# Row maxima of two heads in one unit: two PSUM banks read by one VectorE instruction, in a one-core attention and mixture-of-experts layer

## The chip, the cores and the metric

The kernel runs on one core of one Trainium2 chip. The metric is the time of one execution on the device in microseconds (us), the median of the runs. TensorE (PE) multiplies matrices into PSUM, VectorE (DVE) and ScalarE (ACT) read PSUM, GpSimd (POOL) works on SBUF, and SyncE (SP) issues the transfers. PSUM has eight banks of 512 float32 columns on 128 partitions. Semaphores order the engines, and each engine runs its own list of instructions in the order in which it is written.

## What is computed

The layer adds to x the output of two attention branches, which both take the layer norm of x, and of a mixture of experts. Each attention branch has 16 heads of width 16, on 2 batches of 2048 tokens, with a causal mask:

```
scores = jnp.einsum('bqhd,bkhd->bhqk', Q, K) / math.sqrt(D_K)
scores = jnp.where(causal, scores, -jnp.inf)
attn = jax.nn.softmax(scores, axis=-1)
out = jnp.einsum('bhqk,bkhd->bqhd', attn, V).reshape(Bx, Sx, N_HEADS * D_K)
```

The change touches only the largest score of each row, which the softmax subtracts before the exponential.

## The kernel before

The program has stages one behind the other: projections (`stage_a`), attention of both branches (`stage_b`, the stage of the change), the output projections and the router, and the experts. `stage_b` works on G = 16 groups of GH = 4 heads of one batch.

For a group there are two kinds of score blocks. **M blocks** (`ROW_BLOCKS`, 160 a group) have 128 queries on the partitions and up to 512 keys along the free axis; their only use is the row maximum. A block is (head h, query tile t, key chunk c). Blocks that lie wholly below the diagonal are full (96 a group, 512 wide); those on the diagonal are masked (64 a group, 16 each of width 128, 256, 384 and 512). The list has heads h and h+1 next to each other for the same t and c, so blocks 2n and 2n+1 have the same width. A pair of heads lies in the two halves of the partitions of `qs` and `ks`. **S blocks** (40 key tiles times 4 heads) have keys on the partitions and queries along the free axis; ScalarE takes their exponential into `probs` (line 654), and TensorE multiplies these with the values, the PV product of a key tile (line 634, eight matmuls into `v_bank`), one for the four heads of the tile.

An M block runs like this: TensorE multiplies into one bank of `m_banks` (line 616), and VectorE takes the maximum, a full block by `tensor_reduce` (line 691), a masked one by a `memset` of one column that carries the wait and a `tensor_tensor_reduce` with the mask added (lines 687 and 688, a CUSTOM_DVE row and a short READ_ACCUMULATOR row in the trace). `m_banks` is a ring of MRING = 4 single banks, `s_banks` a ring of SRING = 3, and `v_bank` is one bank: all eight are in use. TensorE's function `room` makes a block wait until the unit four places ahead of it in the ring has been read (`m_used`).

When a 512-query chunk has its last block, VectorE joins the maxima of the chunk (line 697), POOL splits them into two parts (lines 551 and 553), and TensorE transposes them (the **N unit**, line 622, TURN_AFTER = 8 blocks later) into a bank of the same ring; ScalarE copies it out (line 667), and SP puts it into spare rows of `qs`, so that the S matmul subtracts the maximum itself. There are four N units a group.

The order of TensorE's list comes from a table, `TURNS`, one string for each of the 40 key tiles: digits are the S blocks of the four heads, M is one M block, V a PV product. The M blocks run LEAD = 88 blocks ahead of the S blocks: these 88 come alone before the first S block (about 226 to 272 us of the span), and while group g is in its S blocks, M blocks 88 to 159 of g and then 0 to 87 of g+1 are worked on. VectorE has little else to do in this stage.

## Time and profile before

| | |
|---|---|
| median of 3 runs | 2504.02 us (2492.83 to 2504.38) |
| the profiled execution | 2510.96 us |
| its span, first to last instruction | 2509.3 us |
| `stage_b` in the span | about 226 to 1855 us |
| PE busy, whole span | 2314.4 us (92%) |
| DVE busy, whole span | 1893.4 us (75%) |
| ACT busy, whole span | 1516.1 us (60%) |
| mean granted TensorE clock | 0.913 of 2.4 GHz |

Times of rows are from the start of the span. Matmul rows overlap one another, since two matmuls that use different halves of the partitions run side by side and each row holds the way through the array as well; a PE that reads as busy may still have room. The gaps of VectorE and ScalarE are real gaps.

### The profile page before, as it was taken

What the parts mean: (1) busy time and instruction counts of PE and PEld (TensorE: products, weight loads), DVE (VectorE), ACT (ScalarE), POOL (GpSimd) and SP (SyncE); (2) the same over time, 40 slices, a digit from 0 to 9 for tenths busy, and PEclk for the clock granted to TensorE, in tenths of its full rate; (3) what the DMA queues carried; (4) which work ended last, traced back from release to release, by engine and by line L of the source; (5) the groups of instructions that cost most, each with busy time, mean ns of one, the idle gap of its engine ahead of it and who ended that gap; (6) DMA issues with size and microseconds to landing.
All of it is one profiled execution on the core that took longest, in us unless ns stands there. A gap on an engine that the chain in (4) does not pass through costs nothing. (4 is left out here: it accounts for less than half of the span.)

```text
span 2509.3 us, 45515 instructions
## 1 busy us (share of the span) xinstructions
PE 2314.4 (92%) x16105; PEld 1323.9 (53%) x16105; DVE 1893.4 (75%) x5752; ACT 1516.1 (60%) x3189; POOL 505.8 (20%) x403
## 2 busy tenths in 40 slices
PE   5996999999999999999999999999957788999994
PEld 3553444444444444444444444444426688999994
DVE  3544988989989899899989988998707764666672
ACT  2541577778777778787777777787841102454451
POOL 0000001010110110101100100101005113777773
PEclk9996799989989899899989998998987787999997
DMA  5996405425244154253351551641117323666653
GB/s 166 295 243 194 57 5 70 52 36 70 37 52 61 19 75 54 29 70 43 45 70 26 63 61 19 78 52 28 15 34 223 127 84 103 141 132 136 143 124 85
DMA packets 145316, 214.56 MB, mean 86 GB/s; under 512 B 54560, under 2 KB 108000, under 8 KB 136672
## 3 DMA queue, kind: packets, MB, share of 16 engines
q1 hardware_dynamic: 132832, 195.27, 39.4%
q0 software_dynamic: 12288, 16.79, 5.2%
q8 instruction: 109, 1.79, 0.3%
q14 instruction: 87, 0.71, 0.1%
HBM read 138.43 MB, written 76.02 MB: 85 GB/s over the span
## 5 line engine op out<-in xcount | busy, mean ns | idle before, releaser
L654 ACT ACTIVATE probs<-s_banks 128x512 f32<-128x512 f32 (+3 forms) x2560 | 1184.6, 539 | 359.1 <-PE s_banks L605 200.6
L691 DVE TENSOR_REDUCE rowmax<-m_banks 128x1 f32<-128x512 f32 x1536 | 965.6, 682 | 87.5 <-PE m_banks L616 80.4
L605 PE MATMUL s_banks<-qs,ks 50*128 50x512 f32 (+3 forms) x2560 | 866.4, 437 | 15.7 <-ACT probs L654 9.5
L616 PE MATMUL m_banks<-ks,qs 48*128 48x512 f32 (+3 forms) x2560 | 830.6, 448 | 26.2 <-PEq L89 20.5
L634 PE MATMUL v_bank<-probs,vs 128*32 128x512 f32 (+3 forms) x5120 | 637.8, 572 | 1.0 <-ACT probs L654 0.4
L605 PEld LDWEIGHTS s_banks<-qs,ks 50*128 50x128 f32 x2560 | 422.2, 193 | 400.6 <-ACT probs L654 366.7
L616 PEld LDWEIGHTS m_banks<-ks,qs 48*128 48x128 f32 x2560 | 414.7, 197 | 297.3 <-DVE rowmax L691 137.5
L688 DVE CUSTOM_DVE_ANT_0 unused<-m_banks,c_maskq 128x128 bf16<-128x128 f32 (+3 forms) x1024 | 464.6, 486 | 81.1 <-issue 77.7
L551 POOL CAST nparts<-negmax 128x16 fp32r<-128x16 f32 x64 | 12.6, 197 | 1279.5 <-DVE negmax L697 1279.5
L1402 PE MATMUL e_banks<-w_parts,hid_parts 128*128 128x256 f32 x1536 | 188.8, 284 | 1.2 <-issue 0.5
L1402 PEld LDWEIGHTS e_banks<-w_parts,hid_parts 128*128 128x128 f32 x1536 | 185.4, 192 | 1.9 <-DVE hid_parts L1321 1.1
L634 PEld LDWEIGHTS v_bank<-probs,vs 128*32 128x32 f32 x5120 | 103.6, 110 | 154.7 <-issue 79.3
L1387 PE MATMUL e_banks<-xinT,w_parts 128*128 128x512 f32 x768 | 179.2, 393 | 5.1 <-DVE w_parts L1300 5.1
L577 PE MATMUL s_banks<-c_identb,c_later_col_swapped 64*128 64x64 bf16 x1024 | 181.9, 196 | 0.0
L577 PE MATMUL s_banks<-c_identb,c_later_col 64*128 64x64 bf16 x1024 | 177.8, 196 | 0.0
L1387 PEld LDWEIGHTS e_banks<-xinT,w_parts 128*128 128x128 f32 x768 | 144.5, 190 | 35.0 <-issue 5.5
L1355 ACT ACTIVATE hid_parts<-e_banks,c_b1T 128x512 fp32r<-128x512 f32 x128 | 89.6, 700 | 112.7 <-PE e_banks L1387 102.8
L1321 DVE TENSOR_TENSOR hid_parts<-e_hid,hid_parts 128x512 fp32r<-128x512 f32 x128 | 99.0, 786 | 46.3 <-ACT e_hid L1356 46.1
L558 POOL TENSOR_TENSOR rden<-rden,pv_sb 128x2048 f32<-128x2048 f32 x16 | 72.8, 4551 | 196.8 <-DMA rden<-rec_scratch 196.8
L1272 POOL TENSOR_SCALAR scaled<-eout,slot_gates 128x256 f32<-128x256 f32 x64 | 99.4, 1564 | 63.8 <-DVE eout L1331 63.8
L1278 POOL DMA_INDIRECT sum_scratch<-scaled,sums_of x64 | 106.6, 1666 | 19.1 <-issue 14.6
L577 PEld LDWEIGHTS s_banks<-c_identb,c_later_col 64*128 64x128 bf16 x1024 | 90.5, 96 | 27.7 <-issue 13.5
(181 smaller groups left out, 1823.8 us busy)
## 6 DMA issues: line engine op xcount, KB each, us to landing
w<-in_L_ffn_fc_w SPq DMA_DIRECT2D x32, 1024.0 KB, 5.2
qs<-q_scratch SPq DMA_DIRECT2D x96, 256.0 KB, 8.4
ks<-k_scratch SPq DMA_DIRECT2D x96, 256.0 KB, 10.2
q_scratch<-parts SPq DMA_DIRECT2D x64, 256.0 KB, 4.3
k_scratch<-parts SPq DMA_DIRECT2D x64, 256.0 KB, 4.5
v_scratch<-vt SPq DMA_DIRECT2D x16, 512.0 KB, 7.5
v_in<-v_scratch SPq DMA_DIRECT2D x32, 256.0 KB, 10.9
qs<-mrows SPq DMA_DIRECT2D x512, 2.0 KB
```

The lines of the kernel that those rows point to most:

```text
L577: ins = pe.matmul(bank[:, j * HALF:(j + 1) * HALF], const[mask][rows, :], const["identb"][rows, rows], start=False, stop=j == 1)
L605: ins = pe.matmul(bank, ks[rows, slot, h // 2, k * P:(k + 1) * P], qs[rows, slot, h // 2, q * CH + first:(q + 1) * CH], start=True, stop=n ...
L616: pe.matmul(room(("M", NM * group + n))[:, 0:width], qs[rows, slot, h // 2, t * P:(t + 1) * P], ks[rows, slot, h // 2, c * CH:c * CH + wid ...
L634: ins = pe.matmul(v_bank[rows, first:CH], vs[:, slot, k, rows], probs[:, (n * GH + h) % PR, 0:CH - first], start=k == 0, stop=k == TPC * ( ...
L654: act.activation(probs[:, n % PR, 0:width], s_banks[:, (NS * group + n) % SRING, 0:width], ACT.Exp, scale=SCALE).then_inc(p_ready, 1)
L688: dve.tensor_tensor_reduce(unused[:, h, 0:width], scores, const["maskq"][:, CH - width:CH], 1.0, NEG, ALU.add, ALU.max, out).then_inc(m_us ...
L691: dve.tensor_reduce(out, scores, AX.X, ALU.max).then_inc(m_used, 1)
L1272: pool.tensor_scalar(scaled[:, u, j, :], eout[:, u, j, :], slot_gates[:, TPE * e + j:TPE * e + j + 1], None, ALU.mult).then_inc(weighed, 1)
L1278: pool.indirect_dma_start(out=sum_dram, out_offset=bass.IndirectOffsetOnAxis(ap=sums_of[:, TPE * e + j:TPE * e + j + 1], axis=0), in_=scal ...
L1321: dve.tensor_tensor(hid_parts[:, LO, f, :], hid[:, f % HRING, :], f32(hid_parts[:, HI, f, :]), ALU.subtract).then_inc(hid_split, 1)
L1387: last = pe.matmul(banks[:, HBANK + f % HRING, :], w1_parts[:, a, h, f * P:(f + 1) * P], xinT[:, b, h, :], start=h == 0 and (a, b) == PASS ...
L1402: last = pe.matmul(banks[:, OBANK + n, j * D:(j + 1) * D], hid_parts[:, a, f, tile * P:(tile + 1) * P], w2_parts[:, b, f, :], start=f == 0 ...
```

## The change

Heads h and h+1 of the same tile and chunk become one unit. The ring has two places of two banks each instead of four places of one bank. TensorE issues both matmuls of a unit next to each other; the first waits for the whole place, and only the second adds to `m_ready`. A full unit is read by one `tensor_reduce` over both banks (128 x 2 x 512 in, 128 x 2 out). A masked unit is read by two instructions as before, and only the second adds to `m_used`. An N unit takes a whole place of two banks.

```
MRING, SRING = 2, 3
...
-            if group < G:
-                order.append(("M", group, n))
+            if group < G and n % 2 == 1:
+                order.append(("M", group, n // 2))
...
-        ring.append(("M", block))
+        if block % 2 == 1:
+            ring.append(("M", block // 2))
...
-        m_banks = ctx.enter_context(nc.psum_tensor("m_banks", [P, MRING, CH], F32))
+        m_banks = ctx.enter_context(nc.psum_tensor("m_banks", [P, MRING, 2, CH], F32))
...
-                        h, t, c = ROW_BLOCKS[n]
-                        width = min(CH, (t + 1) * P - c * CH)
...
-                        rows = slice(h % 2 * HALF, h % 2 * HALF + PAIR_ROWS)
-                        pe.matmul(room(("M", NM * group + n))[:, 0:width], qs[rows, slot, h // 2, t * P:(t + 1) * P],
-                                  ks[rows, slot, h // 2, c * CH:c * CH + width], start=True, stop=True).then_inc(m_ready, 1)
+                        banks = room(("M", NP * group + n))
+                        for half in range(2):
+                            h, t, c = ROW_BLOCKS[2 * n + half]
+                            width = min(CH, (t + 1) * P - c * CH)
+                            rows = slice(half * HALF, half * HALF + PAIR_ROWS)
+                            ins = pe.matmul(banks[:, half, 0:width], qs[rows, slot, h // 2, t * P:(t + 1) * P],
+                                            ks[rows, slot, h // 2, c * CH:c * CH + width], start=True, stop=True)
+                        ins.then_inc(m_ready, 1)
...
-                        out = rowmax[:, group % SLOTS, h % 2 * PAIRS + h // 2, t, c:c + 1]
-                        scores = m_banks[:, place[("M", NM * group + n)] % MRING, 0:width]
-                        dve.wait_ge(m_ready, NM * group + n + 1)
+                        out = rowmax[:, group % SLOTS, h // 2:h // 2 + PAIRS + 1:PAIRS, t, c]
+                        banks = m_banks[:, place[("M", NP * group + n)] % MRING]
+                        dve.wait_ge(m_ready, NP * group + n + 1)
                         if c == t // TPC:
                             dve.memset(dve_pause[:, h:h + 1], 0.0)
-                            dve.tensor_tensor_reduce(unused[:, h, 0:width], scores, const["maskq"][:, CH - width:CH], 1.0, NEG,
-                                                     ALU.add, ALU.max, out).then_inc(m_used, 1)
+                            for half in range(2):
+                                ins = dve.tensor_tensor_reduce(unused[:, h + half, 0:width], banks[:, half, 0:width],
+                                                               const["maskq"][:, CH - width:CH], 1.0, NEG, ALU.add, ALU.max,
+                                                               rowmax[:, group % SLOTS, half * PAIRS + h // 2, t, c:c + 1])
+                                if half == 0:
+                                    dve.memset(dve_pause[:, h + 1:h + 2], 0.0)
+                            ins.then_inc(m_used, 1)
                         else:
-                            dve.tensor_reduce(out, scores, AX.X, ALU.max).then_inc(m_used, 1)
+                            dve.tensor_reduce(out, banks[:, :, 0:width], AX.X, ALU.max).then_inc(m_used, 1)
```

The table `TURNS` is not touched, but a unit now stands where the second of its two M blocks stood. The first place is on TensorE, in blocks 52 to 55 of a group, behind two PV products (m_banks rows are M blocks, s_banks<-qs,ks rows are S blocks, v_bank rows a PV product). Before:

```order
L605 MATMUL s_banks<-qs,ks 128x512 [waits p_ready]
L634 MATMUL v_bank<-probs,vs 32x512 [waits p_ready,pv_copied]
L634 MATMUL v_bank<-probs,vs 32x512 x3
L616 MATMUL m_banks<-ks,qs 128x512 [waits m_used]
L605 MATMUL s_banks<-qs,ks 128x512 [waits p_ready] x2
L616 MATMUL m_banks<-ks,qs 128x512 [waits m_used] x2
L605 MATMUL s_banks<-qs,ks 128x512 [waits p_ready]
L634 MATMUL v_bank<-probs,vs 32x512 [waits p_ready]
L634 MATMUL v_bank<-probs,vs 32x512 x3
L605 MATMUL s_banks<-qs,ks 128x512 [waits p_ready]
L616 MATMUL m_banks<-ks,qs 128x512 [waits m_used]
```

After:

```order
L607 MATMUL s_banks<-qs,ks 128x512 [waits p_ready]
L639 MATMUL v_bank<-probs,vs 32x512 [waits p_ready,pv_copied]
L639 MATMUL v_bank<-probs,vs 32x512 x3
L607 MATMUL s_banks<-qs,ks 128x512 [waits p_ready] x2
L620 MATMUL m_banks<-ks,qs 128x512 [waits m_used]
L620 MATMUL m_banks<-ks,qs 128x512
L607 MATMUL s_banks<-qs,ks 128x512 [waits p_ready]
L639 MATMUL v_bank<-probs,vs 32x512 [waits p_ready]
L639 MATMUL v_bank<-probs,vs 32x512 x3
L607 MATMUL s_banks<-qs,ks 128x512 [waits p_ready]
L620 MATMUL m_banks<-ks,qs 128x512 [waits m_used]
L620 MATMUL m_banks<-ks,qs 128x512
```

The first M block of a unit has moved down to the second: two rows with one wait on `m_used`, and the S blocks that stood between them are issued ahead of both.

The second place is on TensorE, around the N unit behind block 71 (line 622 before, 627 now). Before:

```order
L616 MATMUL m_banks<-ks,qs 128x512 [waits m_used]
L622 MATMUL m_banks<-c_ident,nparts 32x128 [waits split_ready,m_used]
L605 MATMUL s_banks<-qs,ks 128x128 [waits p_ready]
L577 MATMUL s_banks<-c_identb,c_later_col_swapped 128x64
L577 MATMUL s_banks<-c_identb,c_later_col 128x64
L605 MATMUL s_banks<-qs,ks 128x512 [waits p_ready,mrows_in1]
L577 MATMUL s_banks<-c_identb,c_later_col 128x64
L577 MATMUL s_banks<-c_identb,c_later_col_swapped 128x64
L616 MATMUL m_banks<-ks,qs 128x512 [waits m_used]
```

After:

```order
L620 MATMUL m_banks<-ks,qs 128x512 [waits m_used]
L620 MATMUL m_banks<-ks,qs 128x512
L627 MATMUL m_banks<-c_ident,nparts 32x128 [waits split_ready,m_used]
L607 MATMUL s_banks<-qs,ks 128x128 [waits p_ready]
L579 MATMUL s_banks<-c_identb,c_later_col_swapped 128x64
L579 MATMUL s_banks<-c_identb,c_later_col 128x64
L607 MATMUL s_banks<-qs,ks 128x512 [waits p_ready,mrows_in1]
L579 MATMUL s_banks<-c_identb,c_later_col 128x64
L579 MATMUL s_banks<-c_identb,c_later_col_swapped 128x64
L607 MATMUL s_banks<-qs,ks 128x512 [waits p_ready]
```

Before, block 72 stands five rows behind the N unit and waits for the unit four places ahead of it, block 69. Now the unit of blocks 72 and 73 comes below the rows shown, behind three S blocks with their masks; the place two ahead of it is that of blocks 70 and 71, the unit just ahead of the N unit.

The third place is on VectorE, in the third query tile of the first chunk (512 keys three times for two heads, then a masked block of 384 for each). Before:

```order
L691 TENSOR_REDUCE rowmax<-m_banks 128x1 [waits m_ready] x6
L687 MEMSET dve_pause 128x1 [waits m_ready]
L688 ISA unused,rowmax<-m_banks,c_maskq 128x384
L688 ISA rowmax 128x1
L687 MEMSET dve_pause 128x1 [waits m_ready]
L688 ISA unused,rowmax<-m_banks,c_maskq 128x384
L688 ISA rowmax 128x1
```

After:

```order
L701 TENSOR_REDUCE rowmax<-m_banks 128x2 [waits m_ready] x3
L692 MEMSET dve_pause 128x1 [waits m_ready]
L694 ISA unused,rowmax<-m_banks,c_maskq 128x384
L694 ISA rowmax 128x1
L698 MEMSET dve_pause 128x1
L694 ISA unused,rowmax<-m_banks,c_maskq 128x384
L694 ISA rowmax 128x1
```

Three instructions over two banks stand for six over one. The masked unit keeps its six rows, and its second `memset` no longer waits.

## Rows read from the trace of the kernel before

**Rows 1.** The page: busy tenths of DVE and the clock, 40 slices of the span.

```profile
DVE  3544988989989899899989988998707764666672
...
PEclk9996799989989899899989998998987787999997
```

**Rows 2.** Windows, one group of heads each: columns as the first row names them.

```profile
core 0: us, PE busy (x) PEld busy (x) DVE busy (x) ACT busy (x) POOL busy (x), PEclk, DMA share, GB/s
758.30:860.50 102.20, 101.20 (x776) 45.71 (x772) 88.20 (x293) 76.48 (x170) 12.63 (x11) 0.90 0.38 49
860.50:956.20 95.70, 94.32 (x776) 43.70 (x772) 87.94 (x293) 76.03 (x169) 12.67 (x11) 0.98 0.40 52
956.20:1058.50 102.30, 101.33 (x776) 45.69 (x772) 88.22 (x295) 76.55 (x170) 12.64 (x11) 0.90 0.38 49
1058.50:1154.20 95.70, 94.32 (x776) 43.68 (x772) 87.91 (x294) 76.02 (x170) 12.67 (x11) 0.98 0.42 52
```

**Rows 3.** The page: groups of instructions; count, busy us, mean ns, idle before, releaser.

```profile
L654 ACT ACTIVATE probs<-s_banks 128x512 f32<-128x512 f32 (+3 forms) x2560 | 1184.6, 539 | 359.1 <-PE s_banks L605 200.6
L691 DVE TENSOR_REDUCE rowmax<-m_banks 128x1 f32<-128x512 f32 x1536 | 965.6, 682 | 87.5 <-PE m_banks L616 80.4
...
L634 PE MATMUL v_bank<-probs,vs 128*32 128x512 f32 (+3 forms) x5120 | 637.8, 572 | 1.0 <-ACT probs L654 0.4
```

**Rows 4.** Groups of VectorE by shape, 300 to 1700 us; columns as in rows 3.

```profile
L691 DVE TENSOR_REDUCE rowmax<-m_banks 128x1 f32<-128x512 f32 x1352 | 850.4, 682 | 76.7 <-PE m_banks L616 70.2
L688 DVE CUSTOM_DVE_ANT_0 unused<-m_banks,c_maskq 128x512 bf16<-128x512 f32 x230 | 151.9, 686 | 11.6 <-issue 11.0
L688 DVE CUSTOM_DVE_ANT_0 unused<-m_banks,c_maskq 128x384 bf16<-128x384 f32 x232 | 120.4, 553 | 1.8
...
L688 DVE CUSTOM_DVE_ANT_0 unused<-m_banks,c_maskq 128x128 bf16<-128x128 f32 x228 | 58.9, 285 | 40.2 <-issue 39.5
```

**Rows 5.** Waits in one group of heads: waiting line <- awaited, us in total, times, longest.

```profile
PEld s_banks L605 <- ACT probs L654: 22.3, 41, 0.8
ACT probs L654 <- PE s_banks L577: 10.2, 15, 1.1
ACT probs L654 <- PE s_banks L605: 9.6, 19, 1.3
...
PEld m_banks L616 <- DVE rowmax L691: 7.2, 11, 0.8
PEld m_banks L616 <- DVE rowmax L688: 6.3, 8, 1.2
...
DVE rowmax L691 <- PE m_banks L616: 3.8, 10, 0.8
```

**Rows 6.** Windows, the lead of 88 blocks; columns as in rows 2.

```profile
226.00:272.00 46.00, 44.24 (x87) 22.80 (x87) 45.02 (x128) 0.27 (x1) 6.47 (x5) 0.50 0.02 4
```

**Rows 7.** Timeline of the lead: start, duration (merged), engine, instruction [idle before].

```profile
239.62 3.07 DVE L691 TENSOR_REDUCE rowmax<-m_banks 128x1 f32<-128x512 f32 x5
...
240.35 0.28 PEld L616 LDWEIGHTS m_banks<-ks,qs 48*128 48x128 f32 x1 [0.32 <-DVE rowmax L691]
```

**Rows 8.** Timeline of VectorE, blocks 40 to 55 of group 9.

```profile
1139.00 3.68 DVE L691 TENSOR_REDUCE rowmax<-m_banks 128x1 f32<-128x512 f32 x6
1142.61 0.55 DVE L688 CUSTOM_DVE_ANT_0 unused<-m_banks,c_maskq 128x384 bf16<-128x384 f32 x1
...
1143.30 0.55 DVE L688 CUSTOM_DVE_ANT_0 unused<-m_banks,c_maskq 128x384 bf16<-128x384 f32 x1
...
1144.23 3.68 DVE L691 TENSOR_REDUCE rowmax<-m_banks 128x1 f32<-128x512 f32 x6 [0.37 <-PE m_banks L616]
1147.83 0.69 DVE L688 CUSTOM_DVE_ANT_0 unused<-m_banks,c_maskq 128x512 bf16<-128x512 f32 x1
```

**Rows 9.** Timeline of TensorE beside it: M blocks and two PV products.

```profile
1140.17 0.49 PE L616 MATMUL m_banks<-ks,qs 48*128 48x512 f32 x1
...
1141.41 0.39 PE L616 MATMUL m_banks<-ks,qs 48*128 48x512 f32 x1
...
1142.73 0.44 PE L616 MATMUL m_banks<-ks,qs 48*128 48x384 f32 x1
...
1143.69 0.50 PE L616 MATMUL m_banks<-ks,qs 48*128 48x512 f32 x2
...
1144.94 1.06 PE L634 MATMUL v_bank<-probs,vs 128*32 128x512 f32 x8
...
1146.28 0.62 PE L616 MATMUL m_banks<-ks,qs 48*128 48x512 f32 x2
...
1147.84 0.73 PE L616 MATMUL m_banks<-ks,qs 48*128 48x512 f32 x2
```

17 lines of the change are left out of this document (9 added, 8 removed).

## The prediction, made before the changed kernel was run

> **What bounds the kernel now.** The page's slices come first: VectorE is at 0.8 to 0.9 from slice 5 to slice 27 and the granted clock is near full there [rows 1]. That is the attention stage, some 1630 of 2509 us, and the only one that the change touches. Next come windows of one group of heads each. A group takes 95.7 us where the granted clock averages 0.98 and 102.2 us where it averages 0.90; VectorE is busy 88 us in both, so it has 8 us of gaps in the quick kind, and ScalarE, busy 76, has 20 [rows 2]. TensorE reads 94 of 95.7, but its rows overlap, so that number proves no bound. The groups of instructions show who has the work: 1536 full blocks at 682 ns on VectorE, 2560 exponentials at 539 ns on ScalarE, and PV products that hold TensorE about 1.0 us each [rows 3, 9]. The waits then show that nobody is the bound alone: in one quick group TensorE's queue waits for ScalarE 22.3 us in 41 places and for VectorE 13.5 us in 19, ScalarE waits for TensorE 19.8 us, and VectorE's reduces wait for TensorE 3.8 us [rows 5]. Three engines with in-order lists are held together by the slack in their rings. So the change has to be judged by two things: VectorE's work, and the slack of the ring of `m_banks`.
>
> **Step 1, the merged reduce: a gain.** A reduce lasts 682 ns alone, but back to back the starts are closer: five in 3.07 us give (3.07 - 0.68) / 4 = 598 ns [rows 7]. What widens it is the slope per column, which the masked blocks give: (686 - 285) / 384 columns = 1.044 ns [rows 4]. 512 columns cost 535 ns, so the fixed part of a start-to-start step is 598 - 535 = 63 ns. No two-bank reduce is in the trace. Its price by the slope is 598 + 535 = 1133 ns against 2 x 598 = 1196: 63 ns saved, 768 times, **-48 us**. Bounds: if the merged form gives up the overlap too, it costs 682 + 535 = 1217 ns, +21 ns a pair, +16 us; and if the whole fixed part of a lone reduce, 682 - 535 = 147 ns, went with each second one, -113 us. I take -48, since the row of back-to-back reduces is the nearest. In the lead of 88 blocks VectorE is busy 45.0 of 46.0 us [rows 6] and the gain is real there: 32 pairs, 2 us of the 48. Elsewhere it counts only where VectorE is what the others wait for. The masked blocks keep their instructions; the second `memset` loses a wait on a block that has come with the first, which is worth nothing.
>
> The Trainium skill (Vector Engine (DVE) Microarchitecture Reference, 5.2 Measured stream behaviour on trn2) gives 1.04 ns a column and about 75 ns an instruction after overlap. The rows agree with the slope and show 63 ns; by the page's figure this term would be an estimated 768 x 75 ns = 58 us instead of 48.
>
> **Step 2, VectorE starts a unit only when its second block is there: a loss.** Before, a block that comes late holds up only itself, and TensorE may be up to four blocks (4 x 0.60 = 2.4 us) ahead. Now the first of two blocks is issued where the second stood, VectorE waits for both, and a place is given back only after 1.13 us. TensorE's wait for room stays at the same point of its list: the second block waited for the second block two pairs back, and so does the unit. What changes is how late TensorE may come. With all places in turn, the room comes 1.13 us before VectorE runs dry, and issue, matmul and start take 0.05 + 0.49 + 0.04 = 0.58 us (240.30 to 240.35 in [rows 7]; a matmul in [rows 9]; 1144.19 to 1144.23 in [rows 8, 9]). That leaves 0.55 us; before it was 3 x 0.60 - 0.58 = 1.2 us. A PV product alone holds TensorE 1.0 us.
>
> I walk one stretch with TensorE's times held as they are. VectorE's blocks 40 to 45 start at 1139.00 and 0.60 apart, 46 and 47 at 1142.61 and 1143.30, 48 to 53 from 1144.23, 54 at 1147.83 [rows 8]. The second blocks are issued at 1140.17 (43), 1141.41 (45), 1142.73 (47), 1143.69 (49), 1146.28 (53) and 1147.84 (55), behind PV products at 1144.94 and at 1146.84 [rows 9]. Unit 42/43 is ready at 1140.17 + 0.49 + 0.04 = 1140.70: VectorE, free at 1140.21, waits 0.49 and ends at 1141.83. Unit 44/45 is ready at 1141.84 and ends at 1142.97; 46/47 ready at 1143.21, a wait of 0.24, two masked blocks of 0.49 each (553 ns less 0.06 that overlap the next), end 1144.19; 48/49 ready at 1144.23, end 1145.36; 50/51 end 1146.49; 52/53 ready at 1146.72, a wait of 0.23, end 1147.85; 54/55 ready at 1147.84 + 0.50 + 0.04 = 1148.38, a wait of 0.53. Block 54 then starts 0.55 us later than before, with the gain of five merged reduces (0.31) already in it: a raw loss of 0.86 us in 9.4 us. The stage has some 1630 - 46 us outside the lead, 168 such stretches: raw +144 us if all of it is passed on. It is passed on only where TensorE waits for VectorE, 19 places a group, one in 5 us [rows 5]; elsewhere TensorE sets the pace and VectorE catches up. Bounds 0 and +144; I take half, **+72 us**, because such a place comes about twice in a stretch and the late starts come in about half of it.
>
> **Step 3, the N unit takes a place of two banks: a loss.** The unit behind an N unit waits for the unit just ahead of it, not for one two further back, so VectorE has nothing to read from the end of the one until the other has gone through TensorE: 0.58 us at least, 64 times, 37 us. At a granted clock of 0.5 it is longer. Part of it stands in the trace already as waiting of VectorE, and part may be hidden as in step 2. Bounds 0 and +37, the middle **+19 us**. The copy-out of N by ScalarE frees its place before the next unit but one is due, so I cost that at nothing; if ScalarE is late by an exponential, 0.5 us, it would show there.
>
> **Step 4, TensorE: at nothing.** The same matmuls are issued. The two of a unit use different halves of the partitions and run together (two in 0.50 us at 1143.69 [rows 9]), as an M block and an S block did before. S blocks move ahead of first blocks; ScalarE has 20 us of gaps a group [rows 2] and gains nothing that the end shows. POOL and SP keep their lists.
>
> **The sum.** -48 + 72 + 19 = +43 us. Against the profiled execution of 2511 us that is 2554. The median of the runs is 7 us lower, so the forecast is 2504 + 43 = **2547 us**, slower.
>
> **Rivals.**
> *The ring hides it* (22%). The late second blocks stand where TensorE, not VectorE, sets the pace, and the faster VectorE is early at the next wait. For it: VectorE's gaps are 8 us of 95.7 and ScalarE's 20 [rows 2], so VectorE's work should count. Against: the 0.55 us of slack against a PV product of 1.0 us. Steps 2 and 3 fall to 19 us or less: 2504 - 48 + 19 = 2475.
> *The terms cancel* (17%): step 2 at 30 us instead of 72, 2504 - 48 + 30 + 19 = 2505.
> *The clock falls more often* (12%). Of the four groups shown, two take 6.5 us longer, with more of their time at the lower level of 1.2 GHz (mean 0.90 of 2.4) [rows 2]; I take it that half of the 16 do. A slower feed of TensorE means more pauses in it, and if they bring the long kind to all groups, 8 x 6.5 = 52 us come on top: 2599.
> The Trainium skill (TensorE: Matmul & The Clock Gate, A second HAM failure mode: psum-queue depth-cycling) tells of a kernel in which short idle times between matmul groups, from cycling through the PSUM queue, made the clock go up and down at a cost in throughput. The trace shows the two kinds of groups, but not that the ring is the cause.
> *The two-bank reduce doesn't do what it should* (4%): it costs 1217 ns or more, so step 1 is +16 instead of -48, and the time is 2504 + 16 + 72 + 19 = 2611.
> The forecast itself, slower by 13 to 117 us through late second blocks, has 45%.
>
> **How the numbers follow.** Low end: the first rival with a little less loss, 2470. High end: step 2 in full and step 3 in full, 2504 - 48 + 144 + 37 = 2637, cut to 2620, since not all waits can be passed on. The forecast's own range is 2517 to 2621. A measurement of this kernel can tell about 0.5% (12.5 us) from no change. Faster: the first rival, 0.22. Within: the second, 0.17. Slower: forecast, clock and price, 0.45 + 0.12 + 0.04 = 0.61.
>
> **What would show it.** Step 1: reduces of 128x2 out, 768 of them, with a mean near 1217 ns (starts 1133 ns apart), and VectorE busy some 50 us less. Step 2: VectorE's reduces waiting for `m_banks` matmuls several times the 3.8 us a group, and quick groups of 97 to 100 us instead of 95.7. Step 3: a gap of about 0.6 us in VectorE behind each of the four N units. If the quick groups take 93 us, the ring hid it and I am wrong; if groups at clock 0.90 are 14 or more, the clock did it.

## The result and the profile after

The changed kernel takes 2661.01 us (2653.39 to 2675.29, four runs) against 2498.67 us (2492.83 to 2504.38, four runs) of the kernel before on the same chip: ratio 1.0656 with a 95% interval of 1.06 to 1.0713. It is slower by 162 us, where the prediction said 43 and at most 117 of the same sign. In some experiments part of a kernel's runs took over 1.5% longer at a lower clock, and the ratios and intervals are of its other runs alone. The profiled execution has 2675.29 us, its span is 2673.6 us (before: 2509.3), its mean granted clock 0.883 (before: 0.913).

The page after, slices of VectorE and of the clock, beside [rows 1]:

```profile
DVE  3536886878778778787787877877832783667662
PEclk9995897979979879898897987988987786999997
```

The clock has a 7 or an 8 in the attention stage about every second slice, and VectorE is at 0.7 to 0.8 instead of 0.8 to 0.9. The page's groups of instructions (count, busy us, mean ns, idle before and what ended it), beside [rows 3]:

```profile
L659 ACT ACTIVATE probs<-s_banks 128x512 f32<-128x512 f32 (+3 forms) x2560 | 1189.5, 538 | 506.2 <-PE s_banks L607 307.0
L701 DVE TENSOR_REDUCE rowmax<-m_banks 128x2 f32<-128x1024 f32 x768 | 921.5, 1221 | 184.8 <-PE m_banks L620 180.9
...
L694 DVE CUSTOM_DVE_ANT_0 unused<-m_banks,c_maskq 128x128 bf16<-128x128 f32 (+3 forms) x1024 | 459.7, 486 | 172.9 <-issue 171.2
```

The 768 merged reduces are there, 1221 ns each, 921.5 us busy instead of 965.6. The idle time ahead of the reduces went from 87.5 to 184.8 us, that ahead of the exponentials from 359.1 to 506.2: VectorE has less to do, ScalarE the same, and both wait longer. Two groups of heads after, windows, beside [rows 2]:

```profile
core 0: us, PE busy (x) PEld busy (x) DVE busy (x) ACT busy (x) POOL busy (x), PEclk, DMA share, GB/s
811.10:919.10 108.00, 105.52 (x780) 46.02 (x772) 85.95 (x246) 76.73 (x169) 12.65 (x11) 0.91 0.37 46
919.10:1029.60 110.50, 108.06 (x780) 47.30 (x772) 86.18 (x246) 76.79 (x169) 12.62 (x11) 0.88 0.35 45
```

Before, a quick and a long kind took turns, 95.7 and 102.2 us. Now all are long, and longer than the long kind was. Waits in two groups after (so halve them), beside [rows 5]:

```profile
PEld s_banks L607 <- ACT probs L659: 51.7, 91, 1.7
ACT probs L659 <- PE s_banks L607: 38.6, 47, 2.4
ACT probs L659 <- PE s_banks L579: 25.2, 35, 2.0
DVE unused L694 <- issue: 22.8, 30, 2.4
DVE rowmax L701 <- PE m_banks L620: 22.8, 35, 1.9
...
PEld m_banks L620 <- DVE rowmax L701: 10.8, 16, 1.7
```

The reduces wait 11.4 us a group instead of 3.8, and the masked pairs (their wait is in the `memset` ahead, so it reads as issue) another 11.4. TensorE waits for ScalarE 25.9 instead of 22.3, and ScalarE for TensorE 31.9 instead of 19.8: the same three engines wait for one another, longer. TensorE's wait for room is the exception: 9.9 us a group for VectorE (10.8 and 9.0 in the window of two groups) instead of 13.5.

This compares groups at different clocks. In the kernel before, the group at 0.90 (956.2 to 1058.5 us) already has 6.3 us of such waiting of the reduces and 25.9 of ScalarE. Like for like is smaller; it is read below from groups at full clock.

**How much of it is the clock.** The clock has two levels, 2.4 and 1.2 GHz, so the time at the lower one is 2 x (1 - mean) x time. Before, the long kind has 20.4 us of it and the quick kind 3.8: 16.6 us more at the low level cost 6.5 us, 0.39 us each. Freed from that, both kinds are 94.2 us (the same for both by construction; the windows give the clock to two digits, so 0.39 is good to a few hundredths). After, the groups have 19.4 and 26.5 us at the low level; less 0.39 times that, they are 100.4 and 100.2. Over 16 groups: 6.1 x 16 = 98 us more at equal clock, and (8.95 - 4.75) x 16 = 67 us for more time at the low level, together 165 us. The two profiled executions differ by 164. This is a split by arithmetic from two groups of each kernel; the experiments test both halves, and the whole stage is split at the end. Where the clock falls, before and after, in windows:

```profile
core 0: us, PE busy (x) PEld busy (x) DVE busy (x) ACT busy (x) POOL busy (x), PEclk, DMA share, GB/s
1000.00:1008.00 8.00, 8.00 (x80) 4.79 (x78) 7.65 (x47) 6.22 (x19) 0.42 (x2) 1.00 1.10 128
1008.00:1028.50 20.50, 20.44 (x91) 7.59 (x89) 12.54 (x45) 11.40 (x22) 5.34 (x4) 0.50 0.21 31
1028.50:1040.00 11.50, 11.08 (x92) 5.01 (x94) 10.42 (x29) 9.53 (x20) 6.04 (x2) 1.00 0.32 48
```

```profile
868.00:877.00 9.00, 8.63 (x61) 3.69 (x61) 8.37 (x24) 8.02 (x18) 1.40 (x3) 1.00 0.38 58
877.00:896.70 19.70, 19.65 (x86) 6.96 (x83) 10.04 (x20) 9.18 (x18) 9.99 (x2) 0.50 0.24 32
...
919.10:972.00 52.90, 51.38 (x419) 23.30 (x411) 44.78 (x143) 40.09 (x91) 1.25 (x6) 1.00 0.56 67
972.00:999.00 27.00, 26.60 (x115) 11.18 (x119) 15.16 (x50) 14.74 (x31) 9.17 (x5) 0.51 0.20 32
```

The first fence is the kernel before: the clock falls at 1008 us, at block 157, among the narrow masked blocks at the end of a group's list. The second is the kernel after: the falls are at 877 and 972 us (blocks 13 and 152), and nearly every group has 20 to 27 us at the low level, where before seven of the sixteen had only about 3. VectorE is busy 61% of a low stretch before and 51 to 56% after: everything slows there.

### The profile page after: what moved, and what is told of

It is laid out like the page before. It is cut to its first block and busy times, and to the rows that moved or that the text cites. A ratio compares the mean times of both kernels' runs of the same rounds, so it can differ in the third digit from the quotient of the medians.

```text
span 2673.6 us, 44747 instructions
## 1 busy us (share of the span) xinstructions
PE 2438.8 (91%) x16105; PEld 1343.4 (50%) x16105; DVE 1863.4 (70%) x4984; ACT 1523.2 (57%) x3189; POOL 504.2 (19%) x403
## 5 line engine op out<-in xcount | busy, mean ns | idle before, releaser
L659 ACT ACTIVATE probs<-s_banks 128x512 f32<-128x512 f32 (+3 forms) x2560 | 1189.5, 538 | 506.2 <-PE s_banks L607 307.0
L701 DVE TENSOR_REDUCE rowmax<-m_banks 128x2 f32<-128x1024 f32 x768 | 921.5, 1221 | 184.8 <-PE m_banks L620 180.9
L607 PE MATMUL s_banks<-qs,ks 50*128 50x512 f32 (+3 forms) x2560 | 847.4, 449 | 14.3 <-ACT probs L659 9.9
L620 PE MATMUL m_banks<-ks,qs 48*128 48x512 f32 (+3 forms) x2560 | 716.2, 466 | 59.9 <-DVE rowmax L701 29.8
L639 PE MATMUL v_bank<-probs,vs 128*32 128x512 f32 (+3 forms) x5120 | 672.1, 600 | 1.0 <-ACT probs L659 0.4
L694 DVE CUSTOM_DVE_ANT_0 unused<-m_banks,c_maskq 128x128 bf16<-128x128 f32 (+3 forms) x1024 | 459.7, 486 | 172.9 <-issue 171.2
L620 PEld LDWEIGHTS m_banks<-ks,qs 48*128 48x128 f32 x2560 | 346.2, 206 | 267.9 <-DVE rowmax L701 114.5
L579 PE MATMUL s_banks<-c_identb,c_later_col 64*128 64x64 bf16 x1024 | 170.8, 198 | 0.0
L579 PE MATMUL s_banks<-c_identb,c_later_col_swapped 64*128 64x64 bf16 x1024 | 168.8, 198 | 0.0
L1331 DVE TENSOR_TENSOR hid_parts<-e_hid,hid_parts 128x512 fp32r<-128x512 f32 x128 | 92.8, 738 | 44.0 <-ACT e_hid L1366 43.7
## 6 DMA issues: line engine op xcount, KB each, us to landing
ks<-k_scratch SPq DMA_DIRECT2D x96, 256.0 KB, 10.2
```

What stands on the lines that cost most here:

```text
L579: ins = pe.matmul(bank[:, j * HALF:(j + 1) * HALF], const[mask][rows, :], const["identb"][rows, rows], start=False, stop=j == 1)
L607: ins = pe.matmul(bank, ks[rows, slot, h // 2, k * P:(k + 1) * P], qs[rows, slot, h // 2, q * CH + first:(q + 1) * CH], start=True, stop=n ...
L620: ins = pe.matmul(banks[:, half, 0:width], qs[rows, slot, h // 2, t * P:(t + 1) * P], ks[rows, slot, h // 2, c * CH:c * CH + width], start ...
L639: ins = pe.matmul(v_bank[rows, first:CH], vs[:, slot, k, rows], probs[:, (n * GH + h) % PR, 0:CH - first], start=k == 0, stop=k == TPC * ( ...
L659: act.activation(probs[:, n % PR, 0:width], s_banks[:, (NS * group + n) % SRING, 0:width], ACT.Exp, scale=SCALE).then_inc(p_ready, 1)
L694: ins = dve.tensor_tensor_reduce(unused[:, h + half, 0:width], banks[:, half, 0:width], const["maskq"][:, CH - width:CH], 1.0, NEG, ALU.ad ...
```

## The experiments

The theory going in (A): the start of a pair is late because VectorE waits for its second block and the ring has too little slack (step 2). Rivals: the coarser release of places (B), the clock (C), the order in which TensorE issues the blocks (D), and the merged instruction itself. Each median stands with that of the kernel before on the same chip.

### One part at a time: wait, release, order, reduce

**The wait alone**, on the kernel before:

```
-                        dve.wait_ge(m_ready, NM * group + n + 1)
+                        dve.wait_ge(m_ready, NM * group + (n | 1) + 1)
```

> The kernel before, with one change: VectorE waits for both blocks of a pair before it reads the first. TensorE's order, the ring of four single banks and the release of each bank are as before. Theory A (the loss is that VectorE starts a unit late; my hand walk gave a raw loss of 0.86 us in 9.4 us, 144 us over the stage, of which some part is passed on): 2530 to 2600. Theory B (the loss is the ring, where room comes for two blocks at once and late): 2499 to 2515, since TensorE still gets each bank back singly. Theory C (the clock: any new gap brings the long low stretch to all groups): 2499 + 52 = 2551 or more, with groups of 102 us and a mean clock near 0.89.

Measured: 2572.82 against 2490.99 us, 1.034 (1.026 to 1.042). Windows, two of its groups:

```profile
686.00:785.80 99.80, 95.74 (x776) 42.77 (x772) 88.37 (x294) 77.05 (x169) 12.66 (x11) 1.00 0.39 50
1086.30:1191.30 105.00, 101.11 (x776) 44.64 (x772) 88.67 (x294) 77.39 (x169) 12.65 (x11) 0.93 0.38 48
```

A group at full clock takes 99.8 us, 5.6 more than 94.2, or 16 x 5.6 = 90 us by estimate, against 82 measured. The mean clock is no lower than before (0.919 to 0.932 against 0.915 to 0.928). So this is a loss of structure (more time at the same clock), not of clock, and waiting for the second block is enough to cause one.

**The wait and the release by pairs**, on the kernel before (the wait as above, and):

```
-                    pe.wait_ge(m_used, ring[n][1] + 1)
+                    pe.wait_ge(m_used, (ring[n][1] | 1) + 1)
```

> As the run that waits for both blocks, and TensorE in addition waits for both blocks of a pair to be read before it takes a bank of that pair. Order of TensorE and single place of the N unit as before. Theory A: within 20 us of the run with the wait alone, because a second block's wait for room is where it was. Theory B: most of the loss appears here, 2560 to 2660. If both theories hold a part, half of the loss each.

Measured: 2884.92 us, 1.1613 (1.1513 to 1.1713), clock 0.867, groups of 116 to 130 us. This is outside what either theory gave. With the blocks still spread over TensorE's list, the coarse release makes the first block of a pair wait for a whole pair, and the ring has little slack of this kind.

**The order alone**: the kernel before, single banks, single waits and releases, the first block issued where the second stands:

```
-            if group < G:
+            if group < G and n % 2 == 1:
+                order.append(("M", group, n - 1))
                 order.append(("M", group, n))
```

> The kernel before, with one change: TensorE issues the first block of a pair where the second stood, right ahead of it; VectorE's reads, the four single banks and their release are as before. Theory A: little, 2490 to 2520, since VectorE can still start with the first block and the second is where it was. A rival D (the order of TensorE's list, tuned for single blocks, is what breaks: two blocks with their weight loads at one point, S blocks ahead of them) expects 2550 or more here.

Measured: 1.0523 (1.0412 to 1.0634), some 130 us. The two runs behind this ratio took 2607.96 and 2634.01 us (clock 0.901 and 0.885), two more 2662.50 and 2666.71 us (0.876 and 0.873). The profile is of the one of 2662.50 us. Two of its groups:

```profile
911.00:1020.10 109.10, 108.15 (x780) 48.09 (x772) 88.31 (x293) 76.78 (x169) 12.64 (x11) 0.87 0.35 46
1020.10:1122.90 102.80, 101.53 (x780) 45.74 (x772) 88.16 (x294) 76.57 (x169) 12.70 (x11) 0.95 0.39 48
```

This is what I had costed at nothing. VectorE's instructions and the ring are as before, and most of the loss is there: some 130 us, with an interval of 103 to 158. By the price of the low clock the two groups are 98.0 and 98.8 us at full clock, some 4 more than before, or 16 x 4.2 = 67 us, and the rest is clock.

**The merged reduce undone**: the changed kernel, with a full unit read by two instructions, the second of which releases.

```
-                            dve.tensor_reduce(out, banks[:, :, 0:width], AX.X, ALU.max).then_inc(m_used, 1)
+                            for half in range(2):
+                                ins = dve.tensor_reduce(rowmax[:, group % SLOTS, half * PAIRS + h // 2, t, c:c + 1],
+                                                        banks[:, half, 0:width], AX.X, ALU.max)
+                            ins.then_inc(m_used, 1)
```

> The changed kernel, with each full unit read by two reduces of one bank instead of one over two banks; only the second releases. It takes the merged instruction away and keeps everything else. Its price by the rows is 598 + 598 against 598 + 535 ns, 63 ns for 768 units, 48 us at most: 2661 + 48 = 2709 if VectorE sets the pace, 2661 if TensorE and ScalarE do. With three engines that wait for each other in turn I expect the middle, 2670 to 2700.

Measured: 2671.15 us, 1.0741 (1.0663 to 1.0819). The changed kernel is at 1.0656: the merged instruction gains 10 us by medians and 21 by ratios, which the overlapping intervals don't separate from nothing. It is not the cause of the loss. With the merge undone the full reduces wait 154.2 us for TensorE in the whole span and the masked ones 137.6; with the merge it is 180.9 and 171.2. In these two profiled executions (2667.28 and 2675.29 us) the merge makes VectorE 41 us less busy (1904.1 to 1863.4), and it waits more than that longer.

**Order, wait and release together, in single banks**: both edits above and the order, on the kernel before. Its N unit takes one bank.

```
+                order.append(("M", group, n - 1))
...
+                    pe.wait_ge(m_used, (ring[n][1] | 1) + 1)
...
+                        dve.wait_ge(m_ready, NM * group + (n | 1) + 1)
```

> The kernel before, with all three: both blocks of a pair issued where the second stood, VectorE waits for both, and TensorE waits for both to be read. It lacks only the merged instruction and the two-bank place of the N unit of the changed kernel. Theory D (the place of the blocks in TensorE's list makes nearly all of the loss; the run with that alone gave 2648): the wait and the release add nothing, since both blocks now come together: 2640 to 2670. Theory A or B (ring and wait add their own loss): 2700 or more. The difference to the changed kernel with two reduces (2671) is the N unit's wide place; my price for it was 19 us, 37 at most.

Measured: 2670.99 against 2487.41 us, 1.0765 (1.0675 to 1.0855). Two groups:

```profile
1469.40:1584.30 114.90, 112.35 (x780) 48.37 (x772) 88.94 (x295) 77.38 (x169) 7.18 (x10) 0.84 0.35 44
1584.30:1684.80 100.50, 97.47 (x780) 43.16 (x772) 88.41 (x293) 76.45 (x169) 7.23 (x10) 1.00 0.39 50
```

The same time as with the wide place for N (2671.15, ratio 1.0741), but this doesn't price the wide place. In single banks the second block behind an N unit waits for the block four places ahead, which belongs to the pair just ahead of the N unit, and the release by pairs makes it wait for all of that pair; VectorE waits for this second block. So the same gap stands here (VectorE, block 72 of a group, at full clock):

```profile
709.03 1.29 DVE L692 TENSOR_REDUCE rowmax<-m_banks 128x1 f32<-128x512 f32 x2 [1.26 <-PE m_banks L617]
710.91 1.29 DVE L692 TENSOR_REDUCE rowmax<-m_banks 128x1 f32<-128x512 f32 x2 [0.59 <-PE m_banks L617]
```

At full clock a group takes 100.5 us, what the arithmetic gave for the changed kernel. The other has 36.8 us at the low level for 14.4 us more: 0.39 again. The parts don't add: the wait alone +5.6 us a group, the order alone about +4, all of it +6.3.

### Other orders

**Both blocks where the first stood**, on the kernel before, and the same on the changed kernel:

```
+            if group < G and n % 2 == 0:
+                order.append(("M", group, n))
+                order.append(("M", group, n + 1))
```

> The kernel before, with both blocks of a pair issued where the first stood, so that the second moves up instead of the first moving down. Everything else as before. Theory D1 (what costs is that the first block comes late and VectorE has nothing to read): the loss goes, 2480 to 2530. Theory D2 (what costs is the clump itself, two blocks and a wait for two banks at one point of TensorE's list with S blocks behind them): as slow as the run with the second's place, 2610 to 2670.

```
-            if group < G and n % 2 == 1:
+            if group < G and n % 2 == 0:
```

> The changed kernel, with a unit where the first of its two blocks stood instead of the second. Theory D1: faster than the changed kernel by what the run on the kernel before gains, 2540 to 2600. Theory B (two places of a ring are too few, wherever the unit stands): unchanged or slower, 2650 to 2750, since TensorE now waits for room earlier and holds up the S blocks behind it.

Measured: 2687.67 and 2696.01 us on the kernel before (two more runs 2735.10 and 2750.56 us; no interval), and 2658.39 us on the changed one (1.0693, 1.0619 to 1.0768). Issuing early doesn't help: the changed kernel is no faster by it, at a higher mean clock (0.901 against 0.883), and the other is slower than with the second's place. So "the first block comes too late" doesn't explain the loss of the order. What both places have in common is two M blocks in a row; that this is the reason is argued, not shown.

**Even turns** on the changed kernel:

```
+TURNS = ("0MM12VMM3",) * 40
```

> The changed kernel with another table: each key tile is 0, unit, 1, 2, PV, unit, 3, so that there are two units in every tile, one PV product between any two tiles' units, and neighbours always in different halves of the partitions. Theory D (only the table doesn't fit the units): 2430 to 2500, VectorE's merged reduce gains its 48 us and the late units go. Theory B (the ring is too short for a PV product of 1.0 us whatever the order): 2560 or more.

Measured: 2847.53 and 2859.81 us (two more runs 2932.13 and 2934.82 us; no interval), clock 0.852 in the profiled one. A regular order is no better; it is some 190 us worse than the irregular table.

**A table placed for units.** Perhaps the table only suits single blocks. I placed a new one with units in mind for the changed kernel, and, as the control, one by the same method for the kernel before. (First turns only; all 40 differ.)

```
-TURNS = ("01MM2M3", "0V1MMM2M3V", "0MMM12V3M",
+TURNS = ("M01M23MM", "012MM3", "MM01MVM2M3",
```

> The changed kernel with another table for TensorE's list, in which the units, the S blocks and the PV products are placed for units of two blocks and two places of room; nothing else is changed, and no tile has the same string as before. Theory D (the loss comes from a table that was made for single blocks): most of it goes, 2480 to 2540, near the kernel before or below it. Theory B (two places are too few for a PV product of 1.0 us, whatever the order): 2600 or more. Since all orders so far gave groups of 99 to 102 us at full clock where the kernel before has about 94, I expect about 96 to 97 here, and the rest is the clock's share.

```
+TURNS = ("M01MM23M", "MM01V2MM3MM", "0VM1M2M3VM",
```

> The kernel before, single blocks and four banks, with a table made in the same way for single blocks. A control: if orders made in this way are simply better, part of what the run with the table for units shows is not owed to the units. If the table of the kernel before is near the best for its ring, 2470 to 2510; if it leaves 2 us a group, 2450 to 2475.

Measured: 2708.42 us in one run and 2811.76 to 2830.51 in three, the profiled one (2811.76) among these, for the changed kernel; 2609.68 us (1.0482, 1.0428 to 1.0536) for the control; against 2490.9. One group of each:

```profile
959.70:1079.10 119.40, 118.83 (x777) 50.97 (x773) 86.17 (x245) 76.28 (x168) 12.62 (x11) 0.76 0.33 42
```

```profile
638.00:743.60 105.60, 101.14 (x772) 45.95 (x772) 88.77 (x293) 76.18 (x168) 12.72 (x11) 0.89 0.37 47
```

The method's own table costs the kernel before 119 us, so it tells nothing of the change itself. With 57 us at the low level, 119.40 would be 97 at full clock by the price of 0.39, less than the 100.3 of the changed kernel, but by the 0.33 measured below for groups that are long at the low level it would be 100.5. So whether the order was better at equal clock stays open, and even the quickest run is 47 us slower than the changed kernel.

### Less work on TensorE

If the loss comes from PV products of 1.0 us being longer than the ring's slack of 0.55 us, halving them should help the changed kernel more than the one before. These two kernels leave out the left half of the columns of the PV products of all key tiles but the first of a chunk (and add a constant in the copy-out).

```
+                        left = max(first, CH // 2) if k > 0 else first
...
-                            ins = pe.matmul(v_bank[rows, first:CH], vs[:, slot, k, rows],
-                                            probs[:, (n * GH + h) % PR, 0:CH - first],
+                            ins = pe.matmul(v_bank[rows, left:CH], vs[:, slot, k, rows],
+                                            probs[:, (n * GH + h) % PR, left - first:CH - first],
```

> The kernel before, with PV products of half the columns: for every key tile but a chunk's first, only the queries 256 to 511 of the chunk are multiplied with the values, so that a PV product holds TensorE about 0.57 us instead of 1.0 (and one is added to every sum, so that it stays finite). It leaves that work out. It is the base for the same edit of the changed kernel. VectorE's 88 us a group are the bound that is left: groups near 91 us, 2400 to 2440.

> The changed kernel, with the same short PV products (that work is left out). The changed kernel loses 170 us to the kernel before with full PV products. Theory A/B (a PV product of 1.0 us against 0.55 us of slack in the ring makes the late units): with 0.57 us the loss falls to half or less, 80 us or less to the kernel before with short products, and were the slack all of it, the merged reduce's 48 us would show as a gain. Theory D (the order, whatever the PV product lasts): the loss stays at 120 to 170 us.

Measured: 2585.08 us (1.0356, 1.0285 to 1.0428; the profiled run 2601.55) on the kernel before, clock 0.808, and 2978.11 us (1.1999, 1.1894 to 1.2105) on the changed one, clock 0.678. Both became slower by doing less, and both times are outside what was expected. Two groups of the first and one of the second:

```profile
779.30:867.50 88.20, 86.44 (x774) 45.06 (x775) 86.37 (x293) 76.24 (x169) 12.68 (x11) 1.00 0.45 56
1278.70:1396.40 117.70, 117.17 (x774) 59.44 (x774) 89.04 (x293) 78.93 (x170) 7.21 (x10) 0.62 0.33 42
```

```profile
910.40:1036.70 126.30, 124.04 (x773) 61.53 (x772) 86.41 (x247) 78.53 (x170) 12.64 (x11) 0.62 0.31 39
```

Where the clock stayed full, short products bring a group of the kernel before from 94.2 (estimated above) to 88.2 us, and VectorE has 1.8 us of gaps left: with short products VectorE is nearly the bound. But the clock fell in most groups and took it all back and more. In the changed kernel no group stayed at full clock (0.55 or 0.62 in all ten that were read), so the question that these two were made for stays open.

### More work on TensorE

If the clock is half of the story, unused columns in the narrow blocks should hold it. VectorE reads what it read.

**Wide**: the masked blocks of query tiles 0 to 7 are multiplied 512 wide.

```
+                        if t < 8:
+                            width = CH
```

> The kernel before, with the masked M blocks of query tiles 0 to 7 (blocks 112 to 159 of a group) multiplied 512 columns wide whatever their mask; VectorE reads the same columns as before. More columns stream through TensorE just where its clock falls once a group (blocks 152 to 157). If the clock falls for want of work there, groups of 102 us (20 us at the low level) become groups of 95 to 97: 2440 to 2480, faster than the kernel before. If it falls for another reason, the added columns only cost: 2495 to 2520.

> The changed kernel with the same wide blocks. A group of it has 20 to 27 us at the low level and takes 108 to 110.5 us; by the kernel before (6.5 us for 17 us more at the low level, 0.38 each) it would take 100.2 at full clock. If the wide blocks keep the clock up, 2661 goes to between 2510 and 2600, and what is left over the kernel before with the same edit, some 90 us, is the waiting that the units bring. If the clock share is not real, 2650 to 2680.

**Double**: those of tiles 0 to 3 are 512 wide and multiplied twice into the same bank.

```
+                        if t < 4:
+                            width = CH
...
+                        for again in range(2 if t < 4 else 1):
```

> The kernel before, with the M blocks of query tiles 0 to 3 (blocks 144 to 159) multiplied 512 columns wide and twice over into the same bank: a stronger filler at the narrow place, at some 2 to 3 us of TensorE a group. If the clock falls for want of work, it stays up here too, 2450 to 2500; if the added work delays ScalarE and VectorE by its full time, 2490 + 16 x 3 = 2540.

> The changed kernel with the same doubled blocks. The fall at blocks 152 to 157 goes, the one at block 14 (tile 20) stays or goes with it: between 2540 and 2640. No change (2650 to 2680) if the clock does not follow the filling.

Measured, against 2494.15 us:

| | before | changed |
|---|---|---|
| wide | 2465.0, ratio 0.9883 (0.9822 to 0.9945), clock 0.934 | 2695.78, 1.0845 (1.0765 to 1.0926), clock 0.876 |
| double | 2494.18, 1.0023 (0.9981 to 1.0065), clock 0.940 | 2599.45, 1.0431 (1.0372 to 1.0491), clock 0.917 |

The clock of wide on the kernel before (page), two of its groups, then one of double on the kernel before and two of double on the changed kernel (windows):

```profile
PEclk9996799999999999999999999999768777999997
```

```profile
932.70:1027.50 94.80, 93.56 (x776) 43.53 (x772) 87.89 (x293) 76.04 (x170) 12.67 (x11) 1.00 0.42 52
1027.50:1123.80 96.30, 95.22 (x776) 43.95 (x772) 87.97 (x293) 76.06 (x170) 12.68 (x11) 0.98 0.41 52
```

```profile
1156.70:1253.00 96.30, 94.89 (x792) 44.99 (x789) 88.30 (x294) 76.42 (x169) 7.23 (x10) 1.00 0.42 52
```

```profile
693.40:795.10 101.70, 99.06 (x796) 45.02 (x788) 85.98 (x246) 76.52 (x169) 12.67 (x11) 1.00 0.39 49
795.10:903.50 108.40, 106.27 (x796) 47.28 (x788) 86.09 (x246) 76.83 (x169) 12.63 (x11) 0.92 0.36 46
```

Wide removes nearly all falls of the kernel before up to slice 27 and gains 1.2%, with an interval clear of 1: a group takes 94.8 us at clock 1.00, near the 94.2 of the arithmetic. On the changed kernel the doubled blocks bring some groups back to full clock, at 101.7 us, and give back 62 of the 162 us by medians (56 by ratios). With the same filler in both kernels, 105 us remain (2599.45 against 2494.18), of which 5.4 x 16 = 86 us stand in groups at full clock (101.7 against 96.3). So there is a loss of some 90 us without any fall of the clock, where the arithmetic gave 98, and most of the rest follows the clock. Wide on the changed kernel didn't hold the clock and cost 35 us, against the expectation; why the one filler holds it there and the other doesn't stays open.

### Waits at full clock, and the whole stage split

**Which waits are longer at equal clock.** Groups at full clock, one each (us; before 1058.5 to 1154.2 at 0.98, the others at 1.00: 886.8 to 986.6, 1584.3 to 1684.8, 1431.2 to 1533.0):

| | before | wait alone | all three, single banks | changed, doubled |
|---|---|---|---|---|
| full reduces wait for TensorE | 3.8 | 6.6 | 6.6 | 7.4 |
| TensorE waits for room in `m_banks` | 13.5 | 19.9 | 11.6 | 8.7 |
| TensorE waits for ScalarE | 22.3 | 20.7 | 27.0 | 27.2 |
| ScalarE waits for TensorE | 19.8 | 21.6 | 23.2 | 24.0 |

With the wait alone it is TensorE's wait for room that grows. With the blocks in a row that wait is shorter than before, and TensorE and ScalarE wait longer for each other. The last two columns have the wait for both blocks too; the order alone, which has no group at full clock, shows the same at 0.95 (1020.1 to 1122.9 us): 10.2 us for room, 26.3 for ScalarE, and 25.1 of ScalarE for TensorE.

**The whole stage.** From the first exponential to the last, for seven profiled executions, columns as in [rows 2], in this order: before, wait alone, order alone, all three in single banks, changed, double on the kernel before, double on the changed one:

```profile
275.10:1854.20 1579.10, 1558.52 (x12250) 709.41 (x12249) 1359.63 (x4550) 1218.75 (x2686) 152.91 (x164) 0.94 0.37 47
278.80:1910.10 1631.30, 1567.84 (x12250) 692.29 (x12249) 1365.29 (x4550) 1232.27 (x2687) 153.02 (x164) 0.97 0.36 46
275.90:2007.30 1731.40, 1713.78 (x12250) 759.84 (x12250) 1362.83 (x4550) 1227.31 (x2686) 152.93 (x164) 0.88 0.34 43
279.30:2018.70 1739.40, 1694.20 (x12251) 733.47 (x12250) 1370.84 (x4550) 1230.08 (x2687) 152.72 (x164) 0.90 0.34 43
278.70:2017.60 1738.90, 1697.35 (x12251) 740.05 (x12250) 1328.50 (x3814) 1225.92 (x2687) 152.55 (x164) 0.89 0.34 43
276.70:1836.40 1559.70, 1537.64 (x12506) 721.71 (x12505) 1363.94 (x4550) 1221.54 (x2687) 152.99 (x164) 0.98 0.38 48
277.60:1974.80 1697.20, 1658.06 (x12506) 740.26 (x12506) 1328.97 (x3814) 1226.15 (x2686) 152.95 (x164) 0.94 0.35 44
```

Take 0.39 us off for each microsecond at the low level, 2 x (1 - mean) x time. The rest is the stage at full clock by estimate (good to some 10 us, since the clock has two digits):

| | stage | at the low level | at full clock | over its base |
|---|---|---|---|---|
| before | 1579 | 189 | 1505 | |
| wait alone | 1631 | 98 | 1593 | +88 |
| order alone | 1731 | 416 | 1569 | +64 |
| all three, single banks | 1739 | 348 | 1604 | +99 |
| changed | 1739 | 383 | 1590 | +85 |
| double, before | 1560 | 62 | 1536 | |
| double, changed | 1697 | 204 | 1618 | +82 |

The wait alone is all structure, and has no more time at the low level than the kernel before (whose profiled execution has the lowest clock of its runs); the order alone has 64 us of structure and (416 - 189) x 0.39 = 89 us of clock in its profiled execution (2662.50 us; in the two runs behind its ratio the clock was higher). The changed kernel has 85 us of structure and (383 - 189) x 0.39 = 76 us of clock.

## Why the prediction was wrong

The sign was right, and the mechanism that carried it, the wait for the second block, is real. The size was off, 162 us instead of 43, and the time lies outside the range of 2470 to 2620. The step that failed is step 4, TensorE's order at nothing; with it came the falls of the clock, which the sum left out.

**Step 1, the merged reduce (-48 us): the price right, the worth not.** Two merged reduces in a row take 2.36 us where one takes 1.23, so starts are 1.13 us apart, as the slope gave. Timeline of VectorE after, at the low clock level:

```profile
880.35 0.28 DVE L694 CUSTOM_DVE_ANT_0 unused<-m_banks,c_maskq 128x128 bf16<-128x128 f32 x1 [1.48 <-issue]
...
882.14 2.36 DVE L701 TENSOR_REDUCE rowmax<-m_banks 128x2 f32<-128x1024 f32 x2 [1.28 <-PE m_banks L620]
885.16 1.23 DVE L701 TENSOR_REDUCE rowmax<-m_banks 128x2 f32<-128x1024 f32 x1 [0.66 <-PE m_banks L620]
```

Busy time of the reduces fell by 44 us, and VectorE's by 30 (1893.4 to 1863.4). But undoing the merge costs only 10 us by medians, 21 by ratios. I had written that the gain counts only where VectorE is what the others wait for, and then entered it in full. The rows shown have a gap ahead of each start, and the waits of the run with the merge undone say the same for the whole stage: what the reduces save turns up as longer waiting. The price agrees with the Trainium skill (Vector Engine (DVE) Microarchitecture Reference, 5.2 Measured stream behaviour on trn2): its slope and fixed cost give an estimated 1140 ns for 1024 columns against the 1.13 us of the row.

**Step 2, the wait for the second block (+72 us): the mechanism confirmed.** Alone it measured +82 us. That the size is so near is partly luck: half of a raw 144 us was taken, by a rough count of the places where it is passed on. The signs were as said: the reduces wait 11.4 us a group, three times 3.8, of which about 7 stand at full clock, and groups at full clock take 100 us, at the top of "97 to 100". But step 2 moved the first block down and counted only what VectorE waits for; the move itself loses 130 us with single waits.

**Step 3, the N unit's wide place (+19 us): not tested.** The gap is there, at the block behind an N unit:

```profile
874.20 0.29 DVE L694 CUSTOM_DVE_ANT_0 unused<-m_banks,c_maskq 128x128 bf16<-128x128 f32 x1
...
875.08 1.23 DVE L701 TENSOR_REDUCE rowmax<-m_banks 128x2 f32<-128x1024 f32 x1 [0.59 <-PE m_banks L620]
```

It is 0.59 us long, as forecast. The run in single banks (2670.99 us) and the one with the wide place (2671.15) agree, but both have this gap, so they say nothing of what it costs; the intervals wouldn't show 19 us either.

**Step 4, TensorE's order (nothing): the step that failed.** The argument was that the same matmuls are issued and that ScalarE has 20 us of gaps to spare. The order alone costs some 130 us (1.0523), about half of it (64 to 67 us) at equal clock and the rest through the clock. On top of the wait and with the release by pairs it brings the 82 us of the wait to 184 (1.0765). What it changes is the traffic between TensorE and ScalarE: at full clock ScalarE waits 23.2 and 24.0 us for TensorE instead of 19.8, and TensorE for ScalarE 27 instead of 22.3, while TensorE waits less for room. ScalarE's gaps didn't absorb the new order; they grew. How much of the time each of these waits carries wasn't told apart.

**The clock: a rival that came true on top of the forecast.** I gave 12% to "the long kind in all groups" and 52 us; nearly all groups are of the long kind or longer now, which is 67 or 76 us by arithmetic, and the doubled blocks give back 62. The error was to treat it as an alternative to the forecast instead of a consequence of the order: the wait alone left the clock where it was (0.919 to 0.932), and the order alone brought it to between 0.873 and 0.901. The Trainium skill (TensorE: Matmul & The Clock Gate, A second HAM failure mode: psum-queue depth-cycling) tells of another kernel in which short idle times of TensorE between groups of matmuls made the clock go up and down. That the falls follow TensorE's order and its filling here agrees with it; no run shows that pauses at the ring are their source.

By measured parts, as ratios: order, wait and release together 1.0765 with their share of clock, the wide place untested (1.0741 with it), the merge down to 1.0656, the last two differences within the noise. Order and wait overlap (130 and 82 alone, 184 with the release), so a sum of parts priced alone would have overshot as mine undershot.

**What stays open**: which wait carries the 85 to 98 us at equal clock; what the N unit's place costs; why two M blocks in a row lose time wherever they stand; whether shorter PV products would save the changed kernel at full clock; why a low stretch lasts 3 us in some groups and 20 in others.

## What to carry to other kernels

Where several in-order engines are held together by short rings and an order worked out for them, the order and the size of a unit can be worth more than a faster instruction: here saving 44 us of VectorE's work was worth 10 to 21, and issuing the same matmuls in pairs cost 130. Cost a change of order at more than nothing whenever no engine is the bound alone, and test it by itself first, which takes two lines. Read the granted clock group by group before and after, and when the order of TensorE's list changes, price the clock falls in addition to the waits.

## What the runs showed of the hardware

Less work on TensorE went with a lower granted clock and more time: with about half of the PV columns left out, the kernel before was 3.6% slower and the changed one 12% slower (2978 against 2661 us), at granted clocks of 0.81 and 0.68. And unused columns in the narrow blocks made the kernel before 1.2% faster, at 0.934 to 0.945 instead of 0.915 to 0.933. The same matmuls in another order did as much: 0.873 to 0.901 instead of 0.915 to 0.928. The price of the low level in this stage was steady, 0.35 to 0.39 us for each microsecond spent there in four kernels (before, wait alone, all three, double on the changed one), under the one half that would be lost if the whole stage ran at the pace of TensorE's clock, by the two levels of 2.4 and 1.2 GHz; only with short products was it 0.33.

One reduce over two PSUM banks (128 x 2 x 512) takes 1221 ns where one over a bank takes 682, and two in a row start 1.13 us apart.
